# Fusing the two first terms of a seven-term polynomial projection into one accumulation group per output tile

## The reference

```python
approx_up = hidden_states @ up_w.T                 # 1024 columns
gate_pre = hidden_states @ gate_w.T
delta = gate_pre - local_point
approx_out = approx_up @ local_approx_output.T     # term 0
for idx in range(6):                               # terms 1 to 6
    m = idx + 1
    dterm = exp(log|delta| * m - discount_factor[idx])   # = delta^m / m!, signed
    tmp = dterm * approx_up
    if m > 4:
        tmp = tmp * (|delta| <= 2.5)
    approx_out = approx_out + tmp @ fuse_weight[:, :, idx].T
ffn_out = silu(h @ ffn_gate_w.T) * (h @ ffn_up_w.T) @ ffn_down_w.T
x = layernorm(x + approx_out + ffn_out)
```

## Time and profile before

| | us |
|---|---|
| runs shown (2) | 5277.01 and 5552.05, median 5414.53 |
| profiled execution, its own time | 5298.58 |
| its span, slowest core (core 7) | 5297.0 |
| spans of the 8 cores | 5269.4 to 5297.0 |
| TensorE matmul busy | 4941.0 (93%), 22116 matmuls |
| VectorE busy | 1086.6 (21%) |
| ScalarE busy | 373.2 (7%) |

### The profile page before, as it was taken

How to read it: one execution, slowest core, us unless ns; L and a number is a source line. 1 busy time by engine, 2 the same in 40 slices (tenths; PEclk the granted TensorE clock), 3 DMA queues, 4 the chain that set the end, 5 groups by cost and what they waited for, 6 DMA issues and landing times.

```text
span 5297.0 us, 65229 instructions; the slowest of 8 cores (5269.4 to 5297.0 us)
## 1 busy us (share of the span) xinstructions
PE 4941.0 (93%) x22116; PEld 2163.0 (41%) x22116; DVE 1086.6 (21%) x1746; ACT 373.2 (7%) x596; POOL 1586.5 (30%) x3002
## 2 busy tenths in 40 slices
PE   6999999999999999969759999999999999998894
PEld 2343444444444444324224434444444444443341
DVE  0256200100100100250513561011001001003306
ACT  1010000000000000020101000000000000001101
POOL 3332333333333333313133323333333333332220
PEclk8899999999999999979779999999999999999895
DMA  9999999999999999939689989999999999996692
GB/s 157 127 152 134 151 151 150 153 153 151 153 154 152 149 155 150 138 59 152 110 176 145 153 133 152 153 149 154 153 151 154 153 151 153 153 148 100 99 147 79
DMA packets 452876, 755.36 MB, mean 143 GB/s; under 512 B 48713, under 2 KB 118738, under 8 KB 452562
## 3 DMA queue, kind: packets, MB, share of 16 engines
q0 software_dynamic: 435296, 717.55, 90.1%
q1 hardware_dynamic: 17266, 33.65, 1.9%
HBM read 1451.59 MB, written 16.78 MB: 277 GB/s over the span
## 4 chain that ended last, share of the span: by engine, by line
PE 84%; DVE 6%; DMA 5%; issue 3%; another core or an unknown queue 1%; ACT 1%; POOL 0%; DVEq 0%; POOLq 0%; SPq 0%; ACTq 0%
PE pb L335 80%; DMA wring<-wstream 4%; PE pb L413 2%; DVE acc L595 2%; DVE lnt L592 2%; PE pb L557 1%; DMA acc<-xT 1%; PE pb L562 0%; DVE acc L740 0%; DVE acc L486 0%; POOL wring L310 0%; DVE statA L546 0%; DVE rows L580 0%; DVE pw L458 0%
## 5 line engine op out<-in xcount | busy, mean ns | idle before, releaser
L310 POOL DMA_DIRECT2D wring<-wstream x2994 | 1582.6, 529 | 3588.9 <-PE pb L335 2957.6
L335 PE MATMUL pb<-xbf,wring 128*128 128x512 bf16 x12096 | 2626.5, 380 | 1.9 <-DMA wring<-wstream 1.9
L335 PEld LDWEIGHTS pb<-xbf,wring 128*128 128x128 bf16 x12096 | 1185.5, 98 | 1440.6 <-issue 41.7
L335 PE MATMUL pb<-vsec,wring 128*128 128x512 bf16 x4992 | 1087.0, 379 | 14.8 <-DMA wring<-wstream 13.9
L335 PEld LDWEIGHTS pb<-vsec,wring 128*128 128x128 bf16 x4992 | 483.5, 98 | 617.0 <-issue 48.3
L335 PE MATMUL pb<-tmp,wring 128*128 128x512 bf16 x3072 | 673.0, 382 | 26.1 <-DVE acc L486 25.4
L335 PEld LDWEIGHTS pb<-tmp,wring 128*128 128x128 bf16 x3072 | 300.9, 98 | 397.9 <-issue 44.2
L486 DVE TENSOR_TENSOR acc<-acc,pb 128x512 f32<-128x512 f32 x448 | 300.3, 685 | 632.0 <-PE pb L335 631.5
L413 PE MATMUL pb<-xbf,wring 128*128 128x512 bf16 x1024 | 271.7, 423 | 128.0 <-DMA wring<-wstream 68.4
L538 DVE TENSOR_TENSOR acc<-acc,pb 128x512 f32<-128x512 f32 x256 | 176.0, 688 | 924.6 <-PE pb L335 924.6
L514 DVE TENSOR_TENSOR vsec<-sgB,pb 128x512 bf16<-128x512 f32 x78 | 53.7, 688 | 1025.8 <-PE pb L335 1025.8
(11 more groups left out here) (82 smaller groups left out, 772.5 us busy)
## 6 DMA issues: line engine op xcount, KB each, us to landing
wring<-wstream POOLq DMA_DIRECT2D x2480, 256.0 KB, 5.4
wring<-wstream POOLq DMA_DIRECT2D x448, 128.0 KB, 4.8
acc<-xT SPq DMA_DIRECT2D x2, 8192.0 KB, 43.9
outT<-acc SPq DMA_DIRECT2D x16, 1024.0 KB, 4.3
wring<-wstream POOLq DMA_DIRECT2D x66, 64.0 KB, 5.2
xbf<-xT POOLq DMA_DIRECT2D x4, 1024.0 KB, 14.8
ident_s<-ident SPq DMA_DIRECT2D x1, 64.0 KB
lp_s<-lp_pack SPq DMA_DIRECT2D x1, 4.0 KB
```

The source lines that it names most:

```text
L310: E.dma_start(wring[:, so:so + ccols], ws[:, off:off + ccols]),
L335: return E.matmul(pb[b][:, :], sf(), mf(), start=st_, stop=sp)
```

## The change

Terms 0 and 1 are no longer two loops over the output tiles but one. For each output tile the chunks (m = 0, o) and (m = 1, o) follow each other in the stream, and their 16 matmuls accumulate in one PSUM bank, with one addition into `acc` behind them. The eight chunks of the moving operand of term 1 are all emitted ahead of that loop, after the four last evictions of `delta`; the chunks of term 2 are emitted within it, where those of term 1 and then of term 2 stood. Terms 2 to 6 keep their loops.

```diff
-    for m in range(7):
+    for o in range(c["OC"]):
+        add("sterm", (0, o), c["SC"] * 128, "A")
+        add("sterm", (1, o), c["SC"] * 128, "A")
+    for m in range(2, 7):
         for o in range(c["OC"]):
             add("sterm", (m, o), c["SC"] * 128, "A")
...
+            emit_tmp1_later = []
...
                                 reads=(("pb", sc), "lpn"), writes=(("delta", scg),))
+                            emit_tmp1_later.append(scg)
...
-            for m in range(7):
-                if m == 0:
-                    movbuf, movkey = aubf, lambda kk: ("aubf", kk)
-                else:
-                    bi = (m - 1) % 2
-                    movbuf, movkey = tmpb[bi], (lambda kk, bi=bi: ("tmp", bi, kk))
+            for scg_ in emit_tmp1_later:
+                emit_tmp_chunk(1, scg_)
+            for o in range(OC):
+                chunks = []
+                for m01, movbuf, movkey in (
+                        (0, aubf, lambda kk: ("aubf", kk)),
+                        (1, tmpb[0], lambda kk: ("tmp", 0, kk))):
+                    entry = next_entry("sterm")
+                    assert entry["sel"] == (m01, o)
+                    dret = dma_chunk(entry, ps)
+                    so = dret[1]
+                    items = [((lambda so=so, kk=kk: wring[:, so + kk * 128:so + kk * 128 + 128]),
+                              (lambda kk=kk, movbuf=movbuf: movbuf[:, kk * TP:(kk + 1) * TP]),
+                              movkey(kk)) for kk in range(SC)]
+                    chunks.append((dret, items))
+                bank = (0, 1, 2, 3)[o % 4]
+                tok = mm_group2(bank, chunks)
+                p.v(lambda E, o=o, bank=bank: E.tensor_tensor(
+                    acc[:, o * TP:(o + 1) * TP], acc[:, o * TP:(o + 1) * TP],
+                    pb[bank][:, :], ALU.add),
+                    reads=(("pb", bank), ("acc", o)), writes=(("acc", o),))
+                if o % 2 == 0 and o // 2 < SC:
+                    emit_tmp_chunk(2, o // 2)
+            for m in range(2, 7):
+                bi = (m - 1) % 2
+                movbuf, movkey = tmpb[bi], (lambda kk, bi=bi: ("tmp", bi, kk))
```

## The result

The changed kernel takes 5308.39 us by its median and 5290.81 at the least; the kernel before, measured with it, 5588.46 by its median and 5273.86 at the least. The ratio to the kernel before is 1.0049, 95% interval 1.0035 to 1.0064: 18 to 34 us slower, within the 2% that count as no change here, and on the side that the argument forecast. By cores the kernel before takes 5267.5 us and the changed one 5286.2: 18.7 more (104 and 144 cores, standard error 0.9), against the forecast's 16.5.

A forecast was written before the change was run, and what follows sets the result against it. The prediction took TensorE to set the pace, with the weight ring full. Stall 13.2 us plus slow matmuls 4.0 less DMA 0.7 gave 16.5 us, on 5298.58 a time of 5315.1 us; range 5272 to 5435.

The forecast's parts named there:

- The bound: Whole kernel: weight ring full, TensorE sets the pace; removing 64 additions, 43.8 us of VectorE time, gains nothing.
- Rival A: Terms 0 and 1: additions were on the path after all, 43.8 us go, kernel at 5271.3 us; chance 0.07.
- The wait before the ninth matmul: Start of terms: TensorE waits for all eight term 1 products, 6.4 and 6.8 us, 13.2 us together.
- The chain: ScalarE scalings and VectorE products of term 1: two buffers set the pace, 1.60 us per chunk each, 6.9 us in all.
- The lag: End of the last term 1 product to TensorE's next matmul: 0.24 us.
- The upper bound: Term 1 chain without buffer overlap: 8 x 1.60 = 12.8 us, 5.9 longer; 25 us for both passes.
- The clock: Matmuls behind the stall run at the 1.2 GHz level: 2.0 us per pass, 4 us for two.
- lower bound of nothing: Matmuls behind the stall: clock might keep up, as after waits of 2.3 us in term 4, costing nothing.
- The DMA: Stages of terms 0 and 1: a fuller ring gives back at most 0.7 us of weight waits in pass 0.
- The sum: Whole kernel: 13.2 + 4.0 - 0.7 = 16.5 us more, 5315.1 us on the profiled execution; chance 0.78.
- Rival B: After each stall: a spell of lower granted clock costs 52 us in both passes, 5367 us; chance 0.08, 0.04 beyond 2%.

The follow-up runs named there:

- covered kernel: Changed kernel with term 0 chunks of the first six output tiles put ahead into six PSUM banks; ratio to before 1.0006, undisturbed cores 5269.5 us.
- run with one buffer: Changed kernel with one scaling buffer instead of two for term 1; ratio to before 1.0038, undisturbed cores 5297.7 us.
- half-early run: Changed kernel with the first four term 1 products made during the second half of the gate projection; ratio to before 1.0008, undisturbed cores 5278.8 us.
- stall alone: Kernel before, loops separate, term 1 products all made ahead and term 0's second group waiting for the last; ratio 1.0036, undisturbed cores 5286.6 us.
- covered and spread kernel: Changed kernel with six tiles of term 0 ahead and term 5 chunks prepared every fourth tile of term 4; ratio to before 0.9965, 5240.2 us.

## Why the prediction was right or wrong

**The bound.** "An addition on VectorE after each group costs TensorE nothing there" held: the covered kernel has 32 additions less in the stage of each pass and takes the same 110.4 us. Rival A with its 43.8 us is gone.

**The wait before the ninth matmul.** Right in its place and in its size. Forecast were stalls of 6.4 and 6.8 us; core 4, at the same lower clock in pass 0 as the core of the earlier trace rows, shows 6.22 and 6.59, and core 0 at full clock 6.59 in each. The chain went by its buffers, 1.61 us a pair where 1.60 was put down. The lag from the end of the last product to TensorE was put at 0.24 us; on core 0 it is 197.67 - 196.83 - 0.69 = 0.15. The upper bound, no overlap of the two buffers, is what the run with one buffer shows: 12.4 us each.

**The clock.** Forecast 2.0 us per pass, measured 2.2 (stage less gap). The gap falls between the two rows it was estimated from, and the cost did too. The Trainium skill's rule in TensorE: Matmul & The Clock Gate ("Why this matters for your kernels") warns of such gaps; the rows agree, with 0.42 us per matmul behind each gap of 6.6 us. My lower bound of nothing shows on core 0 of the half-early run, after 3.36 us. One part of the reading of the earlier trace rows needs a remark: the 1.7 us were rightly read as the price of the slow matmuls, but in term 4 they cost no time, since VectorE was the slower there; behind the new gap nothing hides them.

**The DMA.** I credited 0.7 us for a fuller ring. The ring did fill in the gap: on core 0 the queue moved 0 GB/s from 197.6 to 203 us. But the waits for weights lay outside this stage: in it core 0 shows none, with or without the change, so there was nothing to give back; 8.8 us are the gap and the slow matmuls in full.

**The sum.** 16.5 us forecast, 18.7 us on undisturbed cores, 26 by the ratio of slowest cores. What was mis-sized in it is small: the slow matmuls, put at 4.0 us and measured at 4.4, the credit of 0.7 us, of which nothing came, and about 1 us that I can't place.

**Where it went wrong: the scale of the one number.** The time that ends the prediction, 5315.1 us, was formed on the profiled execution's own 5298.58. Beside the median of the two runs shown, 5414.53, it stands 1.8% lower, and so by itself it says faster, while the argument says 16.5 us slower and 0.5% slower was measured. The step that failed is "On the execution's own time: 5298.58 + 16.5 = 5315.1". The text gave the sum on the median too (5431.0) and did not ask which of the two a measurement would be set against. Neither base holds. The two runs lie 275 us apart, so their median stands for neither. The profiled execution had cores 4 to 7 at the lower clock up to 230 us (the earlier trace rows has core 7), and its slowest core took 5297.0 us, against 5267.5 for the undisturbed cores; the lowest times of the kernel before are 5272 to 5274 us in the three measurements. That the changed kernel's median came out at 5308.39, only 7 us from the forecast, is therefore luck: it was taken over all its runs, and the kernel before has 5588.46 by the same count.

**Rival B.** No spell of the lower clock is seen to follow from the stall. In the changed kernel's profile the low spell on core 4 lies where it did on core 7 before: it begins ahead of the change's first instruction and is over by 235 us too:

```profile
64.00:197.00 133.00, 123.11 (x439) 46.50 (x448) 0.00 (x0) 14.33 (x28) 58.38 (x111) 0.80 0.94 108
...
235.00:428.00 193.00, 191.44 (x873) 86.81 (x890) 83.76 (x128) 15.16 (x21) 58.67 (x111) 1.00 1.04 151
```

The Trainium skill, TensorE: Matmul & The Clock Gate, Part 1, tells of a limiter that holds a die at 13/16 while dense matmuls last; here the clock was back at 1.00 with the matmuls as dense as before, and no run here ties the spells to gaps.

## What to carry to other kernels

Ask of each engine's work whether the bound engine waits for it: 44 us of additions under unbroken rows of matmuls were worth nothing, and some 2.5 us of lateness at each of 14 places were worth 34. When two loops are fused, the second loop's operand loses the first loop as its cover; count the chain from its last input to its last piece against what is left to do meanwhile, and, if it is longer, put independent work of the first loop ahead in as many accumulators as are free. When an engine is late, look at the distance between starts and not only at the waits: it tells which engine sets the pace. A forecast in absolute time needs a base made of the runs that it will be compared with.

## What was not expected of the hardware

After a gap of the same length the clock did not always fall. In the half-early run, behind 3.36 us on core 0 the next matmuls took the full pace (granted clock 1.00 from 2808.5 to 2812 us), behind 3.37 us on core 1 sixteen matmuls took 3.0 us more (granted clock 0.50 from 2818 to 2824 us). In term 4 of the kernel before sixteen matmuls took 3.61 us (full pace) behind a gap of 2.01 us and 5.30 behind 2.02; behind 2.31 us they took 5.30 once and 3.61 another time, both on core 1. What decides it no run here shows. Behind 6.6 and 12.4 us every core paid, 2.2 and 2.3 us in the mean.

In the profile of the stall alone cores 4 and 5 ran at the lower clock up to about 520 us; core 4's windows:

```profile
64.00:235.00 171.00, 152.76 (x552) 58.86 (x562) 14.57 (x22) 21.38 (x38) 66.09 (x126) 0.81 0.93 110
235.00:420.00 185.00, 183.75 (x692) 76.68 (x705) 82.72 (x126) 13.71 (x19) 46.64 (x89) 0.81 0.94 124
```

Here the spell was on before the stall came and outlasted it: a stall of 6.4 us (core 4, pass 0) did not end it. Nor does a long spell need a stall: in the profile of the covered and spread kernel, which has none, core 6 stands at 0.81 from 235 to 420 us as well.
